# A decoder layer on one NeuronCore: another order for the beginning, and the row maxima loaded from ScalarE's queue

## The reference

```python
Q = circulant(x, wq_c, wq_b); K = circulant(x, wk_c, wk_b); V = circulant(x, wv_c, wv_b)   # 16 heads of width 8
attn_weights = softmax(einsum('bqhd,bkhd->bhqk', Q, K) * scale)
x = layernorm(x + circulant(attn_weights @ V, wo_c, wo_b))

Sim = (ctx @ w1)[:, :, None] + (x @ w2)[:, None, :] + einsum(ctx * w3, x) + b_sim
hq_hat = softmax(Sim, axis=2) @ ...          # and one row hc_bar, weighted by the softmax of the largest of Sim
x = layernorm(x + concat([enc, hq_hat, enc * hq_hat, enc * hc_bar]) @ W_qv + b_qv)

scores = softmax(x @ gate_w.T)               # the top 2 of 8 experts by scores + gate_b
routed = sum of comb[e] * (swiglu((x @ w1[e] + b1[e]) * (x @ w3[e] + b3[e])) @ w2[e] + b2[e])
x = layernorm(x + routed + shared)           # the shared expert has the same form
```

## Time and profile before

| | us |
|---|---|
| median of 3 runs (lowest to highest) | 418.36 (418.06 to 418.45) |
| the profiled execution's own time | 419.23 |
| its span, first to last instruction | 417.5 |
| first exponential (slot 0) starts | 40.70 |
| TensorE busy | 347.8 (83%) |
| VectorE, ScalarE, GpSimd busy | 282.4, 175.2, 195.5 |
| chain of waits, shares: PE, DVE, issue, DMA, SP's queue | 50%, 19%, 8%, 7%, 6% |

### The profile page before, as it was taken

The page is one execution under the profiler, slowest core; times in us unless marked ns, Lnnn a source line. Parts: engine busy times, 40 slices in busy tenths (PEclk is TensorE's granted clock), DMA queues, the critical chain, the costliest instruction groups (busy, mean ns, idle before and its releaser), DMA issues.

```text
span 417.5 us, 8518 instructions
## 1 busy us (share of the span) xinstructions
PE 347.8 (83%) x2415; PEld 224.0 (54%) x2415; DVE 282.4 (68%) x834; ACT 175.2 (42%) x498; POOL 195.5 (47%) x377
## 2 busy tenths in 40 slices
PE   2637887887998987878978699899999999999790
PEld 1223465665765666556657455455456555555450
DVE  3345477776669887888886866788866666666232
ACT  2122344443443452435452154345555555555313
POOL 9700022224213258753275534346888665656223
PEclk9999999998888999989998699999999999999897
DMA  4774644766726533220002100111322111110063
GB/s 98 172 207 123 196 143 117 209 197 175 207 75 206 156 110 91 64 74 23 23 28 72 63 19 26 40 32 52 90 61 64 54 44 46 45 40 19 27 203 100
DMA packets 53197, 39.56 MB, mean 95 GB/s; under 512 B 7623, under 2 KB 46632, under 8 KB 53147
## 3 DMA queue, kind: packets, MB, share of 16 engines
q1 hardware_dynamic: 50881, 34.33, 29.8%
q0 software_dynamic: 2272, 4.69, 3.4%
HBM read 26.05 MB, written 12.69 MB: 93 GB/s over the span
## 4 chain that ended last, share of the span: by engine, by line
PE 50%; DVE 19%; issue 8%; DMA 7%; POOL 7%; SPq 6%; ACT 2%; ACTq 0%; POOLq 0%; DVEq 0%
PE pT L1501 9%; PE pS L1501 9%; PE pM L1512 5%; DVE negmax L934 3%; PE pO L1492 3%; PE pM L1307 2%; DVE inv_den L950 2%; PE pT L1502 2%; PE pS L1502 2%; PE pT L1478 2%; POOL rstd L614 2%; POOL xs L634 2%; PE pO L1344 2%; PE pT L1331 2%; PE pS L1321 2%
## 5 line engine op out<-in xcount | busy, mean ns | idle before, releaser
L712 POOL DMA_INDIRECT ys<-sim_rhs,row_dest x39 | 40.5, 1038 | 36.7 <-ACT sim_rhs L868 32.8
L766 ACT ACTIVATE PT<-pT 128x512 f32<-128x512 f32 x64 | 38.0, 593 | 36.5 <-PE pT L1331 36.1
L1501 PE MATMUL pT<-W,XH 128*128 (+1 forms) x94 | 50.5, 619 | 0.0
L934 DVE TENSOR_REDUCE negmax<-pS 128x4 f32<-128x512 f32 x64 | 43.4, 679 | 9.0 <-PE pS L1321 8.7
L1501 PE MATMUL pS<-W,XH 128*128 (+1 forms) x94 | 49.0, 604 | 0.0
L612 POOL TENSOR_SCALAR vareps<-meanvar 128x1 f32<-128x1 f32 x32 | 8.5, 264 | 86.6 <-DVE meanvar L963 86.3
L1321 PE MATMUL pS<-Kdiag,Qst 128*128 128x512 f32 x64 | 41.5, 655 | 4.9 <-DMA Kdiag<-parts_scr 4.1
L1071 DVE TENSOR_TENSOR PT<-pT,PT 128x512 f32<-128x512 f32 x47 | 32.4, 690 | 19.4 <-PE pT L1502 16.3
L852 ACT COPY XH<-pO 128x384 f32<-128x384 f32 x47 | 22.5, 479 | 46.6 <-PE pO L1494 39.9
L1512 PEld LDWEIGHTS pM<-W,XH 128*128 128x128 f32 x188 | 28.5, 194 | 18.1 <-issue 14.4
L634 POOL DMA_INDIRECT xs<-X,slot x32 | 33.5, 1048 | 7.5 <-issue 5.2
(11 more groups left out here) (264 smaller groups left out, 823.6 us busy)
## 6 DMA issues: line engine op xcount, KB each, us to landing
parts_scr<-qk_hi SPq DMA_DIRECT2D x16, 256.0 KB, 3.1
W<-in_L_ffn_w SPq DMA_DIRECT2D x16, 256.0 KB, 4.0
Qst<-parts_scr SPq DMA_DIRECT2D x32, 96.0 KB
Kdiag<-parts_scr SPq DMA_DIRECT2D x64, 48.0 KB
Kst<-parts_scr SPq DMA_DIRECT2D x32, 96.0 KB
Qdiag<-parts_scr SPq DMA_DIRECT2D x64, 48.0 KB
sim_add<-xs SPq DMA_DIRECT2D x39, 65.0 KB
parts_scr<-qk_lo SPq DMA_DIRECT2D x8, 256.0 KB, 3.4
```

What stands on the lines that cost most here:

```text
L712: pool.indirect_dma_start(ys.ap(), bass.IndirectOffsetOnAxis(ap=row_dest[:, k:k + 1], axis=0), YO[:, i % RING, :], None).then_inc(s_ysc[i ...
L766: act.activation(PT[:, u % 3, :], pT[:, 0, :], ACT.Exp, scale=SCALE).then_inc(p_sb, 1)
L934: dve.tensor_reduce(out=negmax[:, b % 2, HG * j:HG * (j + 1)], in_=pS[:, u % 2, :].rearrange("p (g k) -> p g k", g=HG), axis=AX.X, op=ALU.max,
L1501: pe.matmul(bank, XH[:, 1 - p, 2 * P:3 * P], W[:, bass.ds(e_up * I2, I2)], start=True, stop=False)
```

## The change

The circulants come in two halves, query and key first, value and output after. The first group's key product goes into a bank of pT, without the wait for the query's low part. The biases of value, output and W_qv and the gate's bias are loaded as one row on one partition, spread by a product with a row of ones (TensorE) and copied by ScalarE to wide_rows. x of group 1 is loaded in the beginning. The context is loaded in four quarters in SP's slots -4, 7, 19 and 35, and each is transposed through pM and scaled in slots 0, 10, 26 and 42. The gate's transpose moves to slot 3. TensorE gets products of ones that nobody reads (`warm`). The two loads of the row maxima are issued by ScalarE, behind the exponential of the slot, and ScalarE waits at its start for c_pool 2. The memset of ones stands first on GpSimd, that of ctx_sb behind the two selects.

```diff
-PREP_SLOT = -11
-X_SLOTS = {-7: 1, 1: 2, 9: 3}
+GATE_SLOT = 3
+CONTEXT_SLOT = -6
+CONTEXT_LOADS = {-4: 0, 7: 1, 19: 2, 35: 3}
+X_SLOTS = {1: 2, 9: 3}
+WARM_UP, WARM_CIRC, WARM_COPY, WARM_STACKS, WARM_SCORES, WARM_MAX = 10, 6, 2, 30, 2, 4
...
+        def context_step(n):
+            q, r = divmod(n - CONTEXT_SLOT, G4 * U)
+            return 0 if n == 0 else q if r == 0 and 1 <= q < NG else None
+        def projection_bank(g, k):
+            return pT[:, 0, :] if (g, k) == (0, 2) else pM[:]
...
         @block.sync
-            for k, c in enumerate((wq_c, wk_c, wv_c, wo_c)):
+            def circ_source(k, c):
                 sp.dma_start(circ_scr.ap()[k].rearrange("(r n) -> r n", r=2),
-                             bass.AP(c.tensor, 0, [[0, 2], [1, D]])).then_inc(s_circw, 16)
+                             bass.AP(c.tensor, 0, [[0, 2], [1, D]])).then_inc(s_circw if k < 2 else s_qkb, 16)
+            def circ_read(half):
+                sp.wait_ge(s_circw, 32)
+                if half == 1:
+                    sp.wait_ge(s_qkb, 64)
+                sp.dma_start(hankel[:, 2 * half:2 * half + 2, :],
+                             bass.AP(circ_scr, 4 * D * half + 1, [[1, P], [2 * D, 2], [1, D]])).then_inc(s_circ[half], 16)
+            circ_source(0, wq_c)
+            circ_source(1, wk_c)
...
-            sp.wait_ge(s_circw, 64)
-            sp.dma_start(hankel, bass.AP(circ_scr, 1, [[1, P], [2 * D, 4], [1, D]])).then_inc(s_circ, 16)
-            sp.dma_start(ctx_sb[1:NC1], ctx_1024.rearrange("b j d -> j b d")).then_inc(s_ctx, 16)
-            sp.wait_ge(c_zero, 2)
-            small = [(bv_row[:], bass.AP(wv_b.tensor, 0, [[0, P], [1, D]])), (bo_row[:], bass.AP(wo_b.tensor, 0, [[0, P], [1, D]])),
+            circ_source(2, wv_c)
+            circ_source(3, wo_c)
+            circ_read(0)
+            circ_read(1)
+            sp.wait_ge(c_zero, 3)
+            small = [(one_row[:, D * k:D * k + r.shape[0]], r.rearrange("(o n) -> o n", o=1)) for k, r in enumerate((wv_b, wo_b, b_qv, gate_b))]
...
                 sp.dma_start(to, src).then_inc(s_small, 16)
+            load_x(1)
...
             for n in range(FIRST_SLOT, LAST_SLOT + 1):
-                if n >= -3 and n % U == 1 and (n + 3) // U < B:
-                    max_rows((n + 3) // U)
...
+                if n in CONTEXT_LOADS:
+                    q = CONTEXT_LOADS[n]
+                    sp.dma_start(ctx_sb[1:NC1, G4 * q:G4 * q + G4, :],
+                                 ctx_1024[G4 * q:G4 * q + G4].rearrange("b j d -> j b d")).then_inc(s_x[q], 16)
...
         @block.scalar
             def group(g, k):
...
+                    if (g, k) == (0, 2):
+                        act.wait_ge(gwT_ps, 1)
+                        act.copy(wide_rows[:], pX[:, 0, 0:3 * D + E]).then_inc(gwT_sb, 1)
+            def max_rows(b):
+                act.wait_ge(mxT_sb, b + 1)
+                if b >= 2:
+                    act.wait_ge(sT_ps, U * (b - 1))
+                for part in range(2):
+                    act.dma_start(Qdiag[RQ + part:RQ + part + 1, b % 2, :, :, :].rearrange("p j g n -> p (j g) n").bitcast(F32),
+                                  maxT[H * part:H * (part + 1), b % 2, :]).then_inc(s_maxrow[b % 2], 16)
             def front(n):
...
+                if n == 0:
+                    context(0)
...
                 if 0 <= n < U * B:
                     exps(n)
+                if n >= -3 and n % U == 1 and (n + 3) // U < B:
+                    max_rows((n + 3) // U)
                 for b, k in late:
                     chain(b, k)
...
+            act.wait_ge(c_pool, 2)
             act.wait_ge(c_ident, 2)
             act.copy(ident_r[:], ident[:]).then_inc(c_identr, 1)
             for n in range(FIRST_SLOT, LAST_SLOT + 1):
-                if n == PREP_SLOT:
-                    act.wait_ge(gwT_ps, 1)
+                if n == GATE_SLOT:
+                    act.wait_ge(gwT_ps, 2)
                     act.copy(gwT[:], pX[:, 1, 0:E]).then_inc(gwT_sb, 1)
-                    for q in range(4):
-                        context(q)
                 front(n)
+                if context_step(n):
+                    context(context_step(n))
...
         @block.vector
+            def circulants(half):
+                dve.wait_ge(circ_ps, half + 1)
+                dve.tensor_copy(circ[:, 2 * half:2 * half + 2, :].rearrange("p k n -> p (k n)"), pX[:, half, 0:2 * D]).then_inc(circ_sb, 1)
...
         @block.tensor
+            def warm(n):
+                for _ in range(n):
+                    pe.matmul(pO[:, 0:P], ones[:], ones[:], start=True, stop=True)
             def group(g, k):
-                projections_free()
+                if (g, k) != (0, 2):
+                    projections_free()
                 if k == 0:
...
+                    if g == 0:
+                        warm(WARM_CIRC)
                 else:
                     if g == 0 and k == 1:
-                        pe.wait_ge(s_circ, 16)
                         pe.wait_ge(c_flip, 2)
-                        pe.matmul(pX[:, 0, :], flip, hankel.rearrange("p k n -> p (k n)"), start=True, stop=True).then_inc(circ_ps, 1)
+                        circulants(0)
+                        warm(WARM_COPY)
                         pe.wait_ge(circ_sb, 1)
                     pe.wait_ge(xT_sb, g + 1)
-                    pe.matmul(pM[:], circ[:, k - 1, :], XT[:, g % 2, :], start=True, stop=True).then_inc(qk_ps, 1)
+                    pe.matmul(projection_bank(g, k), circ[:, k - 1, :], XT[:, g % 2, :], start=True, stop=True).then_inc(qk_ps, 1)
                     issued["qk"] += 1
+                    if (g, k) == (0, 2):
+                        circulants(1)
+                        pe.wait_ge(s_small, 16 * SMALL)
+                        pe.matmul(pX[:, 0, 0:3 * D + E], ones[0:1, :], one_row[:], start=True, stop=True).then_inc(gwT_ps, 1)
+                        warm(WARM_STACKS)
+            def context(q):
+                projections_free()
+                if q == 0:
+                    pe.wait_ge(c_pad, 1)
+                    pe.wait_ge(s_small, 16 * SMALL)
+                pe.wait_ge(s_x[q], 32)
+                for c in range(G4):
+                    mm = pe.transpose(pM[:, c * NC1:(c + 1) * NC1], ctx_sb[:, G4 * q + c, :], ident[0:NC1, 0:NC1])
+                mm.then_inc(cT_ps, 1)
+                issued["t"] += 1
             def front(n):
...
+                if n == 0:
+                    context(0)
                 if 0 <= n + LEAD < U * B:
                     scores(n + LEAD)
+                    if n < 0:
+                        warm(WARM_SCORES)
                 if n >= -3 and n % U == 1 and (n + 3) // U < B:
                     max_transposes((n + 3) // U)
+                if n == 0:
+                    warm(WARM_MAX)
...
+            pe.wait_ge(c_zero, 1)
+            warm(WARM_UP)
```

More of the change, by code:

```diff
@@ L104, in decoder_layer @@
         qk_bias = sb("qk_bias", [P, 2])
[L105 to L108, removed]
+        wide_rows = sb("wide_rows", [P, 3 * D + E])
+        bv_row, bo_row, bqv_row = (wide_rows[:, k * D:(k + 1) * D] for k in range(3))
+        one_row = sb("one_row", [1, 3 * D + E])
         ctx_sb = sb("ctx_sb", [NC1, B, D])
@@ L452, in q_diag @@
                                  parts_of(b, 0, hg)).then_inc(s_qdiag[b % 2], 16)
[L454 to L460, removed]
-                                 maxT[H * part:H * (part + 1), b % 2, :]).then_inc(s_maxrow[b % 2], 16)
             def up_weights(e, done):
@@ L562, in _ @@
         def _(pool):
+            pool.memset(ones[:], 1.0).then_inc(c_zero, 1)
+            pool.memset(ident[:], 0.0).then_inc(c_ident, 1)
+            pool.memset(flip, 0.0).then_inc(c_flip, 1)
             pool.memset(bsim[:], 0.0).then_inc(c_zero, 1)
-            pool.memset(ident[:], 0.0).then_inc(c_ident, 1)
-            pool.memset(ctx_sb[0:1], 0.0).then_inc(c_pad, 1)
-            pool.memset(flip, 0.0).then_inc(c_flip, 1)
-            pool.memset(ones[:], 1.0)
             pool.memset(pad_row[:], 0.0).then_inc(c_zero, 1)
@@ L574, in _ @@
                                pattern=[[1, P]], channel_multiplier=1).then_inc(c_flip, 1)
+            pool.memset(ctx_sb[0:1], 0.0).then_inc(c_pad, 1)
             pool.memset(Kst[:].bitcast(F32), 1.0)
@@ L758, in group @@
                         act.wait_ge(s_parts[i], 48 * g)
-                    act.activation(qk_hi[:, i, :], pM[:], ACT.Identity, bias=qk_bias[:, i:i + 1],
+                    act.activation(qk_hi[:, i, :], projection_bank(g, k), ACT.Identity, bias=qk_bias[:, i:i + 1],
                                    scale=1.0).then_inc(hi_sb, 1)
+                    if (g, k) == (0, 2):
+                        act.wait_ge(gwT_ps, 1)
+                        act.copy(wide_rows[:], pX[:, 0, 0:3 * D + E]).then_inc(gwT_sb, 1)
             def exps(u):
@@ L1231, in _ @@
             dve.memset(Kdiag[:].bitcast(F32), 0.0).then_inc(c_kdiag, 1)
-            dve.wait_ge(circ_ps, 1)
```

(27 more changed lines are left out.)

46 lines of the change are left out of this document (26 added, 20 removed).

## The result

Over 20 runs of each on one chip the changed kernel took 419.95 us (416.75 to 425.24), the kernel before 417.83 (415.08 to 422.16): ratio 1.0052 [1.0028, 1.0077]. The forecast was 412.3, the range 405.5 to 417.0. Wrong in size and in sign.

The account below looks back on a forecast made before the run. Bound: a beginning mostly waiting until 40.7 us, then slots paced by a chain of short steps, then unchanged expert tiles. 419.23 - 4.75 - 1.6 + 2.1 - 1.8 - 1.5 + 1.5 = 413.2, as median 412.3; range 405.5 to 417.0.

Parts of the forecast that it names:

- The query projection at 11.75: Beginning: the query projection would start at 11.75 us instead of 12.10, after XT, delayed by the memset of Qdiag.
- Kdiag issued at 22.4: Beginning: the Kdiag load would be issued at 22.4 us instead of 24.57, once the last spill landed, 3.87 after issue.
- Scores at 25.7: Beginning: the first scores would start at 25.7 us instead of 27.8, following the earlier Kdiag load.
- Bring the level up before the scores: Beginning: thirty warm-up products, 7 to 14 us, in the wait after the key product would raise TensorE's clock before the scores.
- Scores to first exponential: Beginning: row maxima, loads, values and the first context quarter would take from scores at 25.7 to the first exponential at 35.95.
- The term of -4.75: Beginning: the first exponential would come at 35.95 us instead of 40.70, winning 4.75 us (ends -2.5 and -7).
- Slots 0 to 3 at the higher level, -1.6: First four slots: less-max and value products would run at the higher TensorE clock, winning 1.6 us (0 to -3).
- Context quarters, +2.1: Slots 10, 26 and 42: quarters 1 to 3 moved there would cost 0.7 us each, 2.1 in all (0 to 6).
- The maxima, -1.8 and -1.5: Slots, batch 6: maxima issued on ACT would end TensorE's wait to 100.24, -1.8 us, and the slow clock after it, -1.5.
- ACT's queue, +1.5: Slots: maxima issues on ACT would delay work behind them, 0.1 us a batch over 15 batches, +1.5 (0 to 18).
- rival 2: Slots: nothing won from the maxima, transfers colliding as before; without -1.8 and -1.5 the time is 415.6 us; chance 0.15.
- Rival 1: Slots: ACT pays for its issues, costing the chain 0.8 us a batch, 12 instead of 1.5, giving 422.8; chance 0.10.

Follow-up runs that it names:

- e5: Changed kernel, ScalarE's early wait kept, but TensorE makes the query and key circulants before it waits for XT; ratio to the kernel before 1.0003.
- e1: Changed kernel with ScalarE's wait for c_pool 2 moved from its start to just before the first load of the maxima; ratio to the kernel before 0.9905.
- e10: Changed kernel with 46 instead of 30 warm-up products in the wait for Kdiag, ScalarE's early wait kept; ratio to the kernel before 0.9990.
- e3: Kernel before with one edit: ScalarE (ACT) issues the loads of the maxima instead of SP; ratio to the kernel before 0.9997.
- e4: Changed kernel without any warm-up product; ratio to the kernel before 1.0103.
- e8: e1 with context quarter 0 made in slot 4 instead of slot 0; ratio to the kernel before 0.9891.
- e12: e7 without the transposes and scaling of context quarters 1 to 3, loads kept, all batches using quarter 0; ratio to the kernel before 0.9884.
- the three pairs: Three kernels with the new beginning, each with the maxima loads issued by ACT and by SP; ratios lean toward ACT by 0.2, 0.65 and 0.3%.
- e7: e1 with 46 instead of 30 warm-up products in the wait for Kdiag; ratio to the kernel before 0.9877.
- e2: e1 with the loads of the maxima back on SP and no ScalarE wait for c_pool; ratio to the kernel before 0.9970.
- e9: Changed kernel with the loads of the maxima back on SP, ScalarE's early wait kept; ratio to the kernel before 1.0072.

## Why the prediction failed, by its own steps

**The query projection at 11.75: wrong, 13.48.** ScalarE's wait for the memset was seen, with its time (XT forecast at 10.74 + 0.30, copied at 10.98), and then the step "circ is ready by 9 to 10 us" was taken as running beside it. It does not: TensorE waits for XT before it issues the circulant product. 1.73 us lost. e5 puts the product ahead and finds 1.33 of it back (12.15).

**Kdiag issued at 22.4: wrong, 24.97.** 1.7 of the 2.6 is the line above. The rest is the landing of the last spill: issued at 20.27, the issue of Kdiag follows 4.70 later where the prediction took 3.87 (the earlier trace rows have 3.93). In e1 it is 4.81, in e5 4.38 (22.45 - 18.07), in e10 5.72. The prediction named this risk (1.5 MB in flight at once) and kept it only as an end of the range.

**Scores at 25.7: wrong, 29.45.** 2.6 from above; from the first issue of Kdiag to the scores it took 4.48 where 3.23 had been copied from the earlier trace rows. e1 shows 3.14 and e5 4.41, so this landing is not one figure. From the issue of the last spill to the scores, both landings together, it is 7.16 before and 6.88 in e3, against 7.95 in e1, 8.79 in e5, 8.90 in e10 and 9.18 in after: always longer in the new order, with the six spills in a row (7.90 to 9.18 in its twelve traces), and what decides how much stays open.

**"Bring the level up before the scores": wrong.** They did bring it up and were spent too soon. By the earlier trace rows a product is 0.24 at the higher level (2.39 for ten), not 0.22. The thirty lasted 6.96 us, the lower end of the "7 to 14 us" forecast, against a wait of 10.84 (18.61 to 29.45); forecast was 8.35 from the end of the key's low part to the scores, so the gap was there to be seen. After 3.87 idle the first scores are at 0.77; with 46 products and 0.24 idle they are at 0.47 (e10). The Trainium skill (TensorE: Matmul & The Clock Gate, Part 1: The HAM clock gate) puts the penalty of a ramp at under 1% of a typical kernel's span; the runs agree in size (e10 against after 0.6%, e4 against after 0.5%), and the whole difference measured, 0.5%, is no larger.

**Scores to first exponential: 10.25 forecast, 13.54 measured** (12.90 before). About 2.4 of the 3.3 goes with the level (e10 takes 11.17). The other 0.9 is not split; context quarter 0 stands ahead of the first exponential, and in e8, which moves it away, that comes 0.9 before e1's, a difference that single traces also show without such a cause. Sum of these steps: **first exponential 42.99 instead of 35.95**. The term of -4.75 came out as +2.29. With the wait moved (e1) it is 35.98, the forecast's number, but not by its steps: the scores start 2.4 earlier than forecast (23.30 for 25.7), since XT is not held at all, and then take 2.4 longer to the exponential (12.68 for 10.25).

**Slots 0 to 3 at the higher level, -1.6: right.** 9.27 became 7.09, -2.2. Even e4, without any warm-up product, needs 9.48.

**Context quarters, +2.1: not borne out.** Nothing measurable (e12), with 2 us at the edge of what that could tell.

**The maxima, -1.8 and -1.5, and ACT's queue, +1.5: the wait goes, the gain does not come.** The wait for the maxima that ended at 100.24 is gone, a wait of 1.21 for Qdiag's own parts stands in its place (102.22), and slots 22 to 28 take 19.05 instead of 19.90. The window from 100 to 120 us shows a clock of 1.00 where it was 0.79, but that from 80 to 100 shows 0.91 where it was 1.00; over 40 to 225 us it is 0.97 against 0.94, and the slots are no shorter for it. Slots 4 to 22 lose 1.55, and 42 to 63 another 0.5; with the gain from 28 to 42 (1.2) the slots behind the fourth are level: 172.84 in both. By e3 the three terms together are nothing in the kernel before (up to 1.5 us either way), instead of -1.8. That is rival 2, for this kernel as it stood. The Trainium skill (DMA: Bandwidth & Descriptors, Issuing engines are not separate DMA queues) says that issuing from several engines saves only the sequencer's time, usually small beside the transfer, and e3 agrees. The landing did not get shorter: 2.4 us in the median on ACT against 2.0 on SP with all else as before, 2.9 in after. Whether the relief of SP's full queue is worth 1 to 3 us where the slots start early, as the three pairs lean, is open. Rival 1, that ACT pays 0.8 us a batch, is refuted by e3 and by all three pairs: none is slower with ACT as issuer.

**The sum.** The term that turned the sign is that of the beginning, -4.75, and its first wrong step is the circulant product taken to run beside ScalarE's wait. Three single edits there each take the loss away: the wait moved (e1, 0.9905), the order on TensorE (e5, 1.0003), the longer warm-up (e10, 0.9990). Only the first makes the kernel faster than before. By the measured pieces of the profiles: +2.29 at the first exponential, -2.18 in slots 0 to 3, 0.00 from slot 4 to 63, -0.21 in the tiles: -0.10, which is the span's 417.5 to 417.4 and the profiles' equal times. The medians differ by 2.1, 1.4 of it because the profile of before lies above its own median, 0.85 because that of after lies below its own.

**The odds.** The prediction held 0.85 for faster, although it had named the mechanism that undid the gain (ScalarE's wait for the memset), at a price on the good side. No rival had the beginning come late; the list "wrong: a first exponential later than 38" did name where to look.

**Open.** In e1 the lead is 6.83 us at slot 4 and 4.46 at slot 63; 2.0 of the difference goes in slots 22 to 28, where e7 with the same order of work loses none. Whether that is the collision of loads there (DMA share 0.88 in e1's window from 80 to 100 us, 0.70 before, but 0.90 in e7's) or the spread of single runs was not settled. So is which stretches make the medians of before and after differ by more than their profiles do.

## What to carry to other kernels

When a step is moved forward, follow each engine's own program, not only the data: a wait placed first on one engine (ScalarE for a memset) and an order on another (TensorE's wait for XT ahead of work that needs no XT) can join in series and undo it; here one line was worth 1.5% (e1 against after). Size warm-up work by its duration at the higher level and let it end when the awaited load lands; too little by 4 us gave 0.6% away (e10 against after). Before moving a small load to a second queue, look at the wait group that it should remove and at what else arrives just behind: here the group went in every pair, in the new order another load's wait stood in its place, and no gain was clear of the spread.

## What the runs showed of the hardware that was not expected

- The same small load, issued on a second queue, landed later: median 2.9 and longest 7.1 us on ACT in after, 3.1 and 6.7 in e1; 2.0 and 3.5 on SP before, 2.4 and 5.5 on SP in e2. Part of it comes with the denser loads of the new order (e9, on SP with the rest of the change, has 2.1 in the median but 6.6 at the longest), part with the queue (e3 on ACT has 2.4 and 4.7, all else as before).
- The granted-clock column and the durations need both be read: before, the first two windows say 1.00 while the projection takes 2.08 us; in after the column says 0.83 there, with the projection at 1.95, and 1.00 in e1 with 1.13. An idle stretch of 3.87 us ahead of the scores came with products at 0.77 us, one of 3.54 in e1 with 0.47 and 0.77 for a product 1.9 us later, one of 3.56 in e2 with 0.47 throughout.
- From the issue of the first Kdiag load to its use took 3.14 us (e1, e7), 3.18 (e10), 4.41 (e5) and 4.48 (after), though the same spills and loads are issued ahead of it in the same order. Where it took 3.1 to 3.2, the issue itself came 4.8 to 5.7 after that of the last spill; where it took 4.4 to 4.5, 4.4 to 4.7.
